# First convolution of the first group in plain fp32, the split of x moved to the mix stage, x's first loads issued by ScalarE

## The reference, cut to what matters

```python
xc = transpose(x)                                  # features x nodes
h  = relu(bn1(conv1(xc)))                          # conv1: 128x128, one tap
x_conv = relu(bn2(conv2(h)) + xc)                  # conv2: 128x128, 17 taps along the nodes
s  = x @ w_se.T + b_se                             # 3 numbers for each node
A  = exp(-|s_n - s_m|^2) * adj
x_nmp = A @ relu(x @ w_msg.T + b_msg)
gi = concat(x_conv, x_nmp) @ w_ih.T + b_ih
gh = x @ w_hh.T + b_hh
r, z = sigmoid(gi_r + gh_r), sigmoid(gi_z + gh_z)
n  = tanh(gi_n + r * gh_n)
out = layernorm(x + (1 - z) * n + z * x)
```

## Time and profile before

| what | value |
|---|---|
| median of 3 runs | 311.69 us (311.43 to 312.55) |
| the profiled execution | 312.01 us |
| its span | 309.9 us |
| TensorE, VectorE, ScalarE, GpSimd busy in the span | 96%, 80%, 50%, 7% |

### The profile page before, as it was taken

One profiled execution on the slowest core, in us unless ns is written; L12 is line 12 of the kernel. 1 busy time (PEld: TensorE's weight loads), 2 busy tenths in 40 slices (PEclk: granted clock), 3 DMA queues, 4 the chain that ended last, 5 costly groups with the idle time before them and its releaser, 6 DMA issues.

```text
span 309.9 us, 4629 instructions
## 1 busy us (share of the span) xinstructions
PE 296.4 (96%) x1422; PEld 238.1 (77%) x1422; DVE 248.9 (80%) x670; ACT 156.4 (50%) x329; POOL 22.0 (7%) x49
## 2 busy tenths in 40 slices
PE   7799999899999999999999999999999999999981
PEld 5587788688887878888888778888888778888860
DVE  2999978869869969849969969849968996954794
ACT  2784744277775124258755412348764622225445
POOL 3000000000000230000000060000000050000113
PEclk9999999999999999999999999999999999999997
DMA  6602335142103320622213240342211221240002
GB/s 197 253 3 68 136 135 167 43 163 65 54 22 104 122 84 35 212 95 68 68 34 102 68 135 34 132 172 68 68 34 34 67 69 68 78 125 0 0 34 103
DMA packets 12256, 27.22 MB, mean 88 GB/s; under 512 B 1362, under 2 KB 2132, under 8 KB 12116
## 3 DMA queue, kind: packets, MB, share of 16 engines
q1 hardware_dynamic: 12244, 27.08, 26.1%
HBM read 22.88 MB, written 4.19 MB: 87 GB/s over the span
## 4 chain that ended last, share of the span: by engine, by line
PE 85%; DVE 8%; DMA 2%; ACT 2%; issue 1%; POOL 0%; POOLq 0%; SPq 0%; ACTq 0%; DVEq 0%
PE bank L328 81%; DMA xr<-xt_dram 2%; PE bank L526 2%; PE bank L366 1%; DVE first L1108 1%; DVE x_lo L959 1%; DVE H L1074 0%; DVE xr L1295 0%; DVE xr L1300 0%; ACT hn L760 0%; DVE H L1089 0%; DVE first L1114 0%; ACT c_hi L676 0%; DVE x L925 0%; DVE w_hl L933 0%
## 5 line engine op out<-in xcount | busy, mean ns | idle before, releaser
L328 PE MATMUL bank<-V_hi,cw_hi 128*128 128x512 f32 x160 | 70.2, 439 | 1.4 <-DVE V_lo L975 1.4
L328 PE MATMUL bank<-V_lo,cw_hi 128*128 128x512 f32 x160 | 64.5, 403 | 0.0
L328 PE MATMUL bank<-V_hi,cw_lo 128*128 128x512 f32 x160 | 64.4, 402 | 0.0
L328 PE MATMUL bank<-x_hi,w_hl 128*128 128x512 f32 x128 | 47.2, 410 | 2.9 <-DVE x_lo L959 2.9
L328 PEld LDWEIGHTS bank<-V_hi,cw_hi 128*128 128x128 f32 x160 | 30.2, 189 | 9.0 <-DVE V_lo L975 1.6
L328 PEld LDWEIGHTS bank<-V_hi,cw_lo 128*128 128x128 f32 x160 | 30.2, 189 | 8.3
L328 PEld LDWEIGHTS bank<-V_lo,cw_hi 128*128 128x128 f32 x160 | 30.2, 188 | 7.2
L328 PE MATMUL bank<-m_hi,w_hl 128*128 128x512 f32 x96 | 35.2, 399 | 0.0
L328 PE MATMUL bank<-c_hi,w_hl 128*128 128x512 f32 x96 | 35.0, 396 | 0.0
L328 PEld LDWEIGHTS bank<-x_hi,w_hl 128*128 128x128 f32 x128 | 24.1, 188 | 9.7 <-DVE x_lo L959 2.8
L641 ACT ACTIVATE m_hi<-bank 128x512 fp32r<-128x512 f32 x16 | 9.6, 597 | 35.6 <-PE bank L328 35.6
(11 more groups left out here) (136 smaller groups left out, 586.5 us busy)
## 6 DMA issues: line engine op xcount, KB each, us to landing
adj<-adj_dram SPq DMA_DIRECT2D x16, 512.0 KB, 4.6
x<-xt_dram SPq DMA_DIRECT2D x16, 256.0 KB, 3.2
xn<-xn_dram SPq DMA_DIRECT2D x16, 256.0 KB, 4.1
out_dram<-xn SPq DMA_DIRECT2D x15, 256.0 KB, 2.1
xr<-xt_dram SPq DMA_DIRECT2D x13, 256.0 KB, 3.6
xn<-wcv_dram SPq DMA_DIRECT2D x1, 1024.0 KB, 7.8
xr<-xt_dram SPq DMA_DIRECT2D x1, 768.0 KB, 6.4
EF<-wsm_dram SPq DMA_DIRECT2D x1, 512.0 KB, 3.2
```

Source lines behind the costliest of these rows:

```text
L328: return nc.tensor.matmul(out, lhs, rhs, start=start, stop=stop, skip_group_check=True)
```

## The change

The first group's conv1 becomes four plain fp32 matmuls (`conv1_first`) on x as loaded, in place of twelve fp32r matmuls on split halves. Ten of the 14 warm matmuls stand before the first of them and four behind it. The four splits of the first group's x leave the head (there ScalarE made hi of chunks 0 and 1 and VectorE hi of chunks 2 and 3 and all four lo) and go into the first mix stage in two pairs, with all four hi halves on ScalarE; they read x from its second load. x's first two loads are issued by ScalarE on its own DMA queue as its first instructions, where SyncE had issued them between `first` and bmsg. The head's list on ScalarE now has each `h3_hi` right behind its `relu1`; on VectorE `h3_lo` of 1 and 2 stands behind the sum `tapsum[4]`, then `setup_sum(1,0,2)`, the early differences of chunks 0 and 1 and `h3_lo` 3, and only then `setup_sum_lo(4)` and `setup_last_tap_lo`.

```diff
-WARM = 14
+WARM = 10, 4
@@ SyncE
             sp.dma_start(first[:, :], first_d[:, :]).then_inc(first_loaded, 16)
-            load_xs(0, 0)
-            rest = xr[:, 1:4, :].rearrange("p k n -> p (k n)")
-            sp.dma_start(rest, xt_d[0, :, CH:]).then_inc(xs_loaded[1], 16)
@@ TensorE
+            def conv1_first(k):
+                pe.wait_ge(xs_loaded[min(k, 1)], 16)
+                mm(conv1_first_bank[k][:, :], w_first, xr[:, k], start=True, stop=True).then_inc(conv1_done, 1)
...
             pe.wait_ge(warm_ready, 2)
-            warm(WARM)
-            pe.wait_ge(small_ready, 1)
-            for k in range(NC):
-                conv1(0, k, True)
+            warm(WARM[0])
+            pe.wait_ge(first_loaded, 16)
+            conv1_first(0)
+            warm(WARM[1])
+            for k in (1, 2, 3):
+                conv1_first(k)
...
             mix_stage(0, True)
             pe.wait_ge(gatesw_ready, 1)
+            pe.wait_ge(x_ready, NC)
@@ ScalarE
             def split_x(g, k, first):
                 if first:
-                    act.wait_ge(xs_loaded[min(k, 1)], 16)
-                    src = xr[:, k]
+                    act.wait_ge(x_loaded[k], 16)
+                    src = chunk(x, k)
...
                 relu2(g, 0)
+                if first:
+                    split_x(0, 0, True)
+                    split_x(0, 1, True)
                 weights(g, 6)
                 shared(g, 2, first)
                 relu2(g, 1)
+                if first:
+                    split_x(0, 2, True)
+                    split_x(0, 3, True)
                 weights(g, 7)
...
+            act.dma_start(xr[:, 0], xt_d[0, :, 0:CH]).then_inc(xs_loaded[0], 16)
+            rest = xr[:, 1:4, :].rearrange("p k n -> p (k n)")
+            act.dma_start(rest, xt_d[0, :, CH:]).then_inc(xs_loaded[1], 16)
             act.wait_ge(first_loaded, 16)
             nc.scalar.activation(w_hi[:, 0, :], w_first, ACT.Copy).then_inc(whi_ready, 1)
-            split_x(0, 0, True)
-            split_x(0, 1, True)
...
+            act.wait_ge(warm_ready, 3)
             act.wait_ge(bn1_ready, 1)
             relu1(0, 0, True)
             h3_hi(0, 0)
             for k in (1, 2, 3):
                 relu1(0, k, True)
+                h3_hi(0, k)
             act.wait_ge(tapsum_ready, 1)
             sum_hi(4)
             nc.scalar.activation(cw_hi[:, TAPS - 1:TAPS, :], last_tap, ACT.Copy).then_inc(cwhi_ready, 1)
-            for k in (1, 2, 3):
-                h3_hi(0, k)
@@ VectorE, head
             setup_small()
-            split_x(0, 0, True)
-            dve.wait_ge(xs_loaded[1], 16)
-            for k in (2, 3):
-                step(nc.vector.tensor_copy(chunk(x_hi, k), xr[:, k]))
-            for k in (1, 2, 3):
-                split_x(0, k, True)
             setup_messages()
             h3_lo(0, 0)
             dve.wait_ge(taps_loaded, 32)
             setup_sum(0, 0, 1)
             step(setup_sum(3, 2, 3))
             TT(tapsum[4], tapsum[0], tapsum[3], ALU.add).then_inc(tapsum_ready, 1)
+            for k in (1, 2):
+                h3_lo(0, k)
             setup_sum(1, 0, 2).then_inc(tapsum_ready, 1)
+            for k in (0, 1):
+                early_differences(0, k)
+            h3_lo(0, 3)
             setup_sum_lo(4, 1)
             setup_last_tap_lo(2).then_inc(cw_ready, 1)
-            for k in (1, 2, 3):
-                h3_lo(0, k)
-            for k in (0, 1):
-                early_differences(0, k)
```

More of the change, by code:

```diff
@@ L333, in three, with conv1 @@
                 return mm(out, w_l, v_h, stop=stop)
-            def conv1(g, k, first=False):
+            def conv1_first(k):
+                pe.wait_ge(xs_loaded[min(k, 1)], 16)
+                mm(conv1_first_bank[k][:, :], w_first, xr[:, k], start=True, stop=True).then_inc(conv1_done, 1)
+            def conv1(g, k):
                 pe.wait_ge(x_ready, 4 * g + k + 1)
-                if k >= 1 and not first:
+                if k >= 1:
                     pe.wait_ge(h_ready, 4 * g + k)
-                out = conv1_first_bank[k] if first else conv1_bank
-                three(out[:, :], w_hi[:, W1, :], w_lo[:, W1, :], chunk(x_hi, k), chunk(x_lo, k),
+                three(conv1_bank[:, :], w_hi[:, W1, :], w_lo[:, W1, :], chunk(x_hi, k), chunk(x_lo, k),
                       True, True).then_inc(conv1_done, 1)
@@ L900, in setup_small @@
                 nc.vector.memset(rows[:, :, 0:JP], 0.0)
-                nc.vector.memset(rows[:, :, JP + NI:J], 0.0)
+                nc.vector.memset(rows[:, :, JP + NI:J], 0.0).then_inc(warm_ready, 1)
                 nc.vector.memset(f32(U[:, :, :, :, :]), 0.0)
@@ L955, in split_x @@
             def split_x(g, k, first):
-                if not (first and k >= 2):
-                    dve.wait_ge(xhi_ready, 4 * g + k + (1 if first else -1))
-                src = xr[:, k] if first else xs[:, k % 2]
+                dve.wait_ge(xhi_ready, 4 * g + k + 1)
+                src = chunk(x, k) if first else xs[:, k % 2]
                 TT(chunk(x_lo, k), src, f32(chunk(x_hi, k)), ALU.subtract).then_inc(x_ready, 1)
```

## The result

The changed kernel takes 313.86 us (median of 15 runs), the kernel before beside it 312.12 us. One of the 15 runs, 491.88 us at a mean granted clock of 0.56, is left out of the comparison; the mean of the other 14 is 313.43 us against 312.15 us, and the ratio is 1.0042, with a 95% interval of 1.0029 to 1.0055. That is 1.3 us slower, measurably, and within the 0.5% that the prediction called no change. The 14 runs form two groups, seven from 312.48 to 313.11 us and seven from 313.86 to 314.42 us. The profiled execution, 313.96 us with a span of 311.9, is one of the slower group. It is 1.95 us above the profiled execution before.

The account below looks back on a forecast made before the run. TensorE was taken to bound the kernel, with conv2's start and the first mix stage's end as places to act. Head -0.4 and mix +2.0 us gave +1.6, so 311.69 to 313.3 us, range 312.0 to 314.9 us.

Parts of the forecast that it names:

- the gain of the head: Start of conv2's first product: predicted at 15.45 us, 0.4 us earlier than before.
- the term of the mix stage: First mix stage: the moved splits make TensorE lose 2.0 us, bounds 1.2 and 2.4 us.
- The late m_hi: ScalarE, pair 2 of the mix stage: hi halves of chunks 2 and 3 make m_hi 0.8 us late.
- the waits on mask 6, mask 7 and gates_lo: End of the mix stage: TensorE waits about 0.9 us on the first, two more follow, together about 2.0 us.
- T + 4.95: Head, VectorE's chain from the taps: conv2 starts 4.95 us after the last tap lands.
- 0.84 us of early differences: Head, VectorE: the new order puts this work ahead of conv2, where it stood behind its start.
- If the two streams share evenly it lands about when the taps do: Head loads: x's rest, sharing with the taps, lands at 10.3 us by the old count, estimated at 9.5.
- R + 5.95: Head, chain from x: conv2 starts 5.95 us after R, the landing of x's chunks 1 to 3, so at 15.45.
- T: Head: landing of the last tap, estimated at 10.2 us.
- The second queue fills the slow start: Rival in the head, chance 0.17: taps at 9.0, x by 8.0, conv2 at 13.95 us, total 311.8 us.
- sign of being wrong: Head or mix: x's rest lands by 8 us and taps by 9.3, or TensorE passes gather 6 without waiting.
- a fall, to which the prediction gave 0.04: Rival: clock falls to 1.2 GHz in TensorE's 2 us idle before x's rest; 2.5 us reach conv2, total 315.8 us.

Follow-up runs that it names:

- e2: The changed kernel with the four splits of the first group's x moved to idle slots of the first mix stage: 310.72 us, ratio 0.9969 to the kernel before.
- e3: The changed kernel with x's first two loads issued by SyncE in their old place: 315.03 us, ratio 1.0095 to the kernel before.
- e6: The changed kernel with early differences of chunks 0 and 1 behind the lo halves of the summed taps: 311.80 us, ratio 0.9979 to the kernel before.
- e1: The changed kernel with eight more constant matmuls behind the first four messages, before conv2: 312.74 us, ratio 1.0019 to the kernel before.
- e4: The kernel before with only x's first two loads moved to ScalarE's own queue: 311.30 us, ratio 0.9998 to the kernel before.

## Why the prediction was right, and where it was not

The forecast of +1.6 us (313.3) met a measured +1.3 us, but the gain of the head was 0.83 us too small and the cost of the clock was missing. These two errors nearly cancel: that the total came out is in part luck, and only the term of the mix stage is a real hit.

**The mix stage, +2.0 us predicted, 1.85 measured: right in mechanism and size.** The late m_hi (0.9 us after 51.70, part of it since TensorE's list was 0.2 us late), the shortened idle time in front of m_lo, the waits on mask 6, mask 7 and gates_lo came as worked out, the first with 0.75 against 0.85 us. e2 shows that place was the cause, and that VectorE's idle times, of which the prediction counted only the one in front of pair 2, can take up all 2.4 us.

**The head, -0.4 us predicted, -1.23 measured: the landing times were mis-sized.** The chain T + 4.95 held (5.07 in the changed kernel and in e3), and so did the 0.84 us of early differences (0.86 in e6). What failed is the step "If the two streams share evenly it lands about when the taps do". x's rest landed at 7.2 us, not 9.5, and the chain from x, R + 5.95 = 13.15 us, did not bind. By the rates of the stretches above, and some 0.2 MB before 3 us, about 1.7 MB had moved by 7.2 us, of which 1.05 were x and 0.14 `first`; the taps had had about 0.5. That is an estimate. T was 9.53 us, where the forecast had 10.2 and the kernel before 10.90. Of these 1.37 us of gain 0.94 stand in front of the issue (1.97 against 2.91 us) and 0.43 between issue and landing (7.56 against 7.99). The second part is not clear of the spread: with the same loads e1 took 8.00 us to landing and e6 7.54, with one queue e3 took 7.86. No run issued the taps earlier without the second queue, so the two parts are a division of the time and not two causes shown apart. The prediction was not consistent here either: it put the earlier issue at 0.8 us, yet took only 0.7 us off T.

This was nearly the rival "The second queue fills the slow start", to which the prediction gave 0.17: its R of at most 8.0 us came (7.2), the measured T of 9.53 us lies between its 9.0 and the forecast's 10.2, and conv2's start at 14.60 us lies between its 13.95 and the forecast's 15.45. Of the prediction's sign of being wrong, "x's rest lands by 8 us and the taps by 9.3", the first half came and the second missed by 0.23 us.

The rule cited from the Trainium skill ("DMA: Bandwidth & Descriptors", "Rules for kernel authors") gave T = 10.1 us in the prediction. The traces nearly agree with it from 5.5 to 8 us, where two queues move 435 GB/s and one 406, or 414 in e3. Before that they go against it: 176 against 70 GB/s between 3 and 4 us, and 417 (410 in e4) against 190 (280 in e3) between 4 and 5.5 us. There the measurement decides.

**The clock: a fall, to which the prediction gave 0.04, came in half of the runs, in another place.** The prediction looked at the idle time in front of x's rest and named its fall there; with x at 7.2 us that gap closed. It gave no weight to the gap that the same head leaves behind the messages, 2.25 us where 1.43 had been. This costs 1.46 us when it comes; e1 shows the cause, and its runs, all in the range of the faster group, show that it explains the two groups. The Trainium skill ("TensorE: Matmul & The Clock Gate", "Why this matters for your kernels") warns of idle gaps between bursts of matmuls, but of longer ones than this; here the row with 2.25 us decides. The kernel before may not be free of such falls: of its 60 runs beside the experiments ten show a mean granted clock of 0.985 to 0.989 with a span of 310.5 to 311.1 us, where most spans are near 309.9. No trace of one is kept, so where their clock fell is not shown.

**The sum.** -1.23 + 1.85 is +0.62 us, which is the faster group (312.7 us, as e1), and with the fall +2.08, the profiled execution (+1.95). Half and half is +1.35 us, ratio 1.0043. Against the forecast of +1.6 us the head brought 0.83 us more and the mix cost 0.15 us less, and the clock took 0.73 us on average: the right number came from too small a gain in the head, against a clock cost that the forecast had left out.

## What to carry to other kernels

Work moved off the head is free only in the slots where its new engine idles: the same four splits cost 1.85 us in one place and nothing 4 to 11 us earlier. When a head gets faster on its inputs but not at its end, look at what TensorE does in between: an idle gap that grows can cost more in clock than the head won, and a few constant matmuls close it. Ask of two queues how soon they reach the full rate together, not only what they move once they have it. And when a sum comes out right, compare its terms one by one: here two of three were wrong.

## What the runs showed of the hardware

With loads in flight on two queues the 16 engines reached 417 GB/s between 4 and 5.5 us (410 in e4), against 190 with one queue (280 in e3), while the small first load took 4.0 us in place of 2.2 to land. Of idle gaps in front of conv2, those of 1.43 us (the kernel before) and 1.49 us (e6) were followed by no fall of the clock in the profiled executions. Those of 2.25 us (the changed kernel and e2) and 2.55 us (e3) were followed by a granted clock of 0.50 for some 3.4 us, which began 0.6, 1.1 and 1.0 us after the work had resumed. The gap of 2.25 us did so in only half of the changed kernel's runs, going by their times, and in three of e2's 12.
